# DVE's second layer norm in the MLP phase: eight tensor-scalar operations of 96 columns in place of two broadcast operations

## What is computed

```python
def _ln(x, g, b):
    m = jnp.mean(x, axis=-1, keepdims=True)
    v = jnp.mean(jnp.square(x - m), axis=-1, keepdims=True)
    return (x - m) * jax.lax.rsqrt(v + EPS) * g + b
xs = jnp.roll(x, shift=(-SHIFT, -SHIFT), axis=(1, 2))
# win: xs in windows, (windows, 64 tokens, 96)
h = _ln(win, ln1_g, ln1_b)
q, k, v = (jnp.einsum('ntc,chd->nthd', h, w) + b for w, b in ((wq, bq), (wk, bk), (wv, bv)))
attn = jax.nn.softmax(jnp.einsum('nqhd,nkhd->nhqk', q, k) / np.sqrt(KD), axis=-1)
win = win + jnp.einsum('nqhd,hdc->nqc', jnp.einsum('nhqk,nkhd->nqhd', attn, v), wo) + bo
h2 = _ln(win, ln2_g, ln2_b)
win = win + jax.nn.gelu(h2 @ w1 + b1, approximate=False) @ w2 + b2
# and back: windows to image, roll by (+SHIFT, +SHIFT)
```

## Time and profile before

| what | value |
|---|---|
| time of 3 runs | 5121.0, 5121.04, 5125.81 us; median 5121.04 us |
| span of the profiled execution | 5118.4 us, 275139 instructions |
| PE busy | 4931.8 us (96%), 103124 instructions |
| PEld busy | 4154.1 us (81%) |
| DVE busy | 4072.6 us (80%), 9254 instructions |
| ACT busy | 3873.0 us (76%) |
| POOL busy | 3623.5 us (71%) |
| DMA | 410.68 MB, mean 80 GB/s |

### The profile page before, as it was taken

The page is one execution under the profiler, slowest core; times in us unless marked ns, Lnnn a source line. Parts: engine busy times, 40 slices in busy tenths (PEclk is TensorE's granted clock), DMA queues, the critical chain, the costliest instruction groups (busy, mean ns, idle before and its releaser), DMA issues.

```text
span 5118.4 us, 275139 instructions
## 1 busy us (share of the span) xinstructions
PE 4931.8 (96%) x103124; PEld 4154.1 (81%) x103124; DVE 4072.6 (80%) x9254; ACT 3873.0 (76%) x8206; POOL 3623.5 (71%) x3589
## 2 busy tenths in 40 slices
PE   7999999999999999999999999999999999999999
PEld 6888888888888888888888888887888888888887
DVE  8969778697786977869788796887968879698786
ACT  7859688595886958769587695976949769496794
POOL 6868667686676866767767677676776767777676
PEclk9999999999999999999999999999999999999999
DMA  3141331313213132131322314223042230422304
GB/s 109 34 119 54 94 94 42 116 48 102 86 48 116 42 111 77 56 113 37 117 74 62 112 33 123 68 68 109 26 123 68 74 108 24 124 65 77 108 26 122
DMA packets 222028, 410.68 MB, mean 80 GB/s; under 512 B 29225, under 2 KB 131850, under 8 KB 221898
## 3 DMA queue, kind: packets, MB, share of 16 engines
q1 hardware_dynamic: 220336, 409.06, 27.0%
q10 hardware_dynamic: 1562, 0.50, 0.0%
HBM read 208.11 MB, written 201.33 MB: 80 GB/s over the span
## 4 chain that ended last, share of the span: by engine, by line
PE 55%; DVE 16%; DMA 9%; issue 8%; SPq 7%; ACT 2%; DVEq 2%; POOL 1%; ACTq 0%; POOLq 0%
PE psum L576 12%; PE psum L702 6%; PE psum L591 6%; PE psum L622 6%; PE psum L651 5%; PE psum L608 5%; PE psum L688 5%; PE psum L637 5%; DMA oT<-turned_rows 5%; DMA turned_rows<-normed 4%; SPq L269 4%; PE psum L544 4%; DVE normed L1002 3%; SPq L275 2%; DVE normed L1009 2%
## 5 line engine op out<-in xcount | busy, mean ns | idle before, releaser
L340 POOL TENSOR_TENSOR probs<-probs,prob_inv 128x512 f32<-128x512 f32 x771 | 783.1, 1043 | 839.6 <-DVE prob_inv L982 836.2
L988 DVE TENSOR_TENSOR stream<-stream,psum 128x384 f32 (+1 forms) x1024 | 547.1, 549 | 298.5 <-PE psum L702 225.0
L750 ACT ACTIVATE normed<-stream,shift,rstd 128x96 f32 (+1 forms) x2072 | 770.5, 461 | 17.8 <-issue 16.1
L902 DVE BATCH_NORM_STATS2 stats<-stream 128x6 f32 (+2 forms) x4224 | 721.3, 243 | 58.0 <-DVE stream L988 29.4
L379 POOL TENSOR_TENSOR rstd<-variance,minus_half 128x8 f32<-128x8 f32 (+2 forms) x201 | 745.0, 3707 | 15.7
L347 POOL TENSOR_TENSOR hT<-hT_upper,hT_lower 96x1024 f32<-96x1024 f32 x258 | 614.2, 2380 | 11.8 <-DVE hT_lower L951 6.8
L702 PEld LDWEIGHTS psum<-w_w,gelu_odd 128*64 128x64 f32 x12288 | 512.4, 137 | 59.4 <-issue 59.4
L974 DVE TENSOR_REDUCE prob_sum<-probs 128x8 f32<-128x512 f32 x771 | 492.5, 678 | 84.2 <-ACT probs L784 84.1
L966 DVE TENSOR_TENSOR probs<-psum,row_max 128x512 f32<-128x512 f32 x771 | 533.2, 692 | 26.6
L830 ACT ACTIVATE gelu_odd<-psum 128x512 f32<-128x512 f32 x768 | 418.7, 593 | 174.8 <-PE psum L688 156.5
L702 PE MATMUL psum<-w_w,gelu_odd 128*64 128x96 f32 x12288 | 536.4, 247 | 12.2 <-ACT gelu_odd L830 12.2
(11 more groups left out here) (94 smaller groups left out, 11327.9 us busy)
## 6 DMA issues: line engine op xcount, KB each, us to landing
turned_rows<-normed SPq DMA_DIRECT2D x624, 128.0 KB
stream<-in_x SPq DMA_DIRECT2D x272, 192.0 KB
out<-stream SPq DMA_DIRECT2D x256, 192.0 KB
stream<-in_x SPq DMA_DIRECT2D x272, 180.0 KB
out<-stream SPq DMA_DIRECT2D x256, 180.0 KB
probsT<-turned_rows SPq DMA_DIRECT2D x112, 384.0 KB, 3.2
oT<-turned_rows SPq DMA_DIRECT2D x112, 384.0 KB, 3.2
turned_rows<-gelu_odd SPq DMA_DIRECT2D x144, 128.0 KB
```

What stands on the lines that cost most here:

```text
L340: nc.gpsimd.tensor_tensor(block_h, block_h, inv, ALU.mult).then_inc(probs_ready, 1)
L750: last = nc.scalar.activation(normed1[:, t, :], stream[:, slot, t * C:(t + 1) * C], ACT.Identity, bias=shift1[:, index, t:t + 1], scale=rs ...
L902: last = nc.vector.bn_stats(stats[:, index, c, :], stream[:, slot, c * C:(c + 1) * C])
L988: nc.vector.tensor_tensor(part, part, psum[:, banks[g], 0:GROUP], ALU.add).then_inc(added, 1)
```

## The change

In `normalise2` of DVE the two operations over 768 columns become eight `tensor_scalar` operations, one for each tile of 96 columns. Each reads its tile of the stream and does both steps, subtraction of the mean and multiplication by rstd, with two operands of one value for each partition. `scale2`, its wait and the semaphore `centre2_step` are gone; `ln2_ready` is incremented by the last of the eight. POOL's own `normalise2`, for units 0 to 2, is as before. The number of DVE's instructions for a unit's norm goes from two to eight; nothing else changes on any engine.

```diff
-        centre2_step = sem("centre2_step")
...
                 wait_apart(dve, h2_turned, u)
                 dve.wait_ge(rstd2_ready, u + 1)
-                nc.vector.tensor_tensor(normed2[:, :, :],
-                                        stream[:, slot_of(u), :].rearrange("p (t c) -> p t c", c=C),
-                                        mean2[:, index, :].unsqueeze(2).to_broadcast((P, TILES, C)),
-                                        ALU.subtract).then_inc(centre2_step, 1)
-
-            def scale2(b, u, index):
-                dve.wait_ge(centre2_step, (BATCH - AHEAD) * b + index - AHEAD + 1)
-                nc.vector.tensor_tensor(normed2[:, :, :], normed2[:, :, :],
-                                        rstd2[:, index, :].unsqueeze(2).to_broadcast((P, TILES, C)),
-                                        ALU.mult).then_inc(ln2_ready, 1)
+                for t in range(TILES):
+                    last = nc.vector.tensor_scalar(
+                        normed2[:, t, :], stream[:, slot_of(u), t * C:(t + 1) * C],
+                        mean2[:, index, t:t + 1], rstd2[:, index, t:t + 1], ALU.subtract, ALU.mult)
+                last.then_inc(ln2_ready, 1)
...
                     normalise2(batch + j + 3, j + 3)
-                    scale2(b, batch + j + 3, j + 3)
                     turn_h2(batch + j + 3, turned_late, False)
```

## The result

The changed kernel takes 5209.83 us (median of 4 runs, 5206.17 to 5217.93) against 5121.51 of the kernel before (median of 4): ratio 1.0173, 95% interval 1.0159 to 1.0188. Its profiled execution took 5206.17 us, with a span of 5201.9, 83.5 us more than the span before.

The account below looks back on a forecast made before the run. TensorE was taken to bound the MLP phases, losing time to DVE's late lower half and ACT's gelu. Unit 11's 0.7 us over 16 phases gave 11 us off 5121: 5110 us, range 5073 to 5140.

Parts of the forecast that it names:

- the rival "slower": GpSimd's additions delay norms uncovered, pushing odd units up to unit 11: 5134 us, 5125 to 5150; chance 26%.
- (b): GpSimd's addition gets in among the eight; DVE waits 1.83 us; hand-off in units 6 and 8 about 3.4, 1.1 more.
- hand-off: Time from the norm's start to the transpose's start; 2.30 us in quiet unit 6 before the change.
- decision points: Hand-offs of 3.2 us in unit 6 and 3.9 in unit 8, from which odd units are pushed, up to unit 11.
- The cover: Slack to hide (b) in unit 6: lower half ready at 2167.13, TensorE asks for it at 2170.17.
- (a): A norm behind a running GpSimd operation has its instructions prepared meanwhile: 0.4 us less in units 3, 9 and 15.
- The number 0.237: Estimated us between starts of the eight on DVE, set by its sequencer's register operations; bounds 0.158 and 0.29.
- the 2.27 us: Forecast hand-off in a quiet unit, against 2.30 before; bounds 1.7 and 2.65; no gain there.
- (c): GpSimd's small statistics steps stop waiting: queue 1.3 us earlier behind units 5, 7, 10; some 0.6 left at unit 11.
- Unit 11: One tensor-scalar, two GpSimd operations, seven tensor-scalars; transpose at 2200.7 instead of 2201.40, 0.7 us per phase.
- The "much faster" rival: DVE's own pace holds, or unit 11 is interrupted once: 31 us off, 5090 us (5070 to 5098); chance 30%.
- the signs named: Expected trace marks, such as 0.24 us pace; wrong if GpSimd waits for all eight or TensorE waits at units 7 to 9.

Follow-up runs that it names:

- e6: Changed kernel with mean and rstd at an index that does not depend on the loop (right statistics left out for units 4 to 15): 5200.7 us, ratio 1.0143.
- e8: Changed kernel with two constants in place of the per-partition mean and rstd: 5121.86 us, ratio 1.0001 to the kernel before.
- e2: Changed kernel with the old two broadcast operations back in even units 4 to 14, the eight in odd units: 5165.39 us, ratio 1.0073.
- e1: Changed kernel, but the eight write normed2 with a one-element gap after every 32 columns: 5054.84 us, ratio 0.9859 to the kernel before.
- e7: Changed kernel with a gap after every 48 columns of normed2 (two parts; output not right): 5206.06 us, ratio 1.0168.
- e10: Changed kernel with GpSimd's lower half done on all 128 partitions instead of 96 (output not right): 5193.44 us, ratio 1.0133.

## The prediction against the runs

**Direction and range were wrong.** 5110 us (5073 to 5140) was forecast, 5209.83 measured; the rival "slower" had 5125 to 5150.

**The step that failed is (b).** That a GpSimd operation would get in among the eight was right, at 1.85 us for 2.52, and that it arrives as the norm begins. It was priced as one addition, 1.83 us of waiting, a hand-off of 3.4. But the earlier trace rows was read one row too short. Behind the addition of unit 6 GpSimd has two more operations ready, in the kernel before as well:

```profile
2153.30 2.52 POOL L436 TENSOR_TENSOR stream<-stream,b_all 128x768 f32 x1 [0.44 <-POOL rstd L379]
2155.79 1.28 POOL L429 TENSOR_TENSOR h2T_even_lower<-probsT,h2T_even_upper 96x512 fp32r<-96x512 f32 x1
2157.03 1.83 POOL L436 TENSOR_TENSOR stream<-stream,b_all 128x768 f32 x1
```

and unit 11 in the earlier trace rows had already shown such a pair go ahead of a waiting DVE operation, for 3.62 us. Together they make 1.83 + 1.25 + 1.83 = 4.9 us, and a hand-off of 6.65 us. So the decision points of the "slower" rival, 3.2 us in unit 6 and 3.9 in unit 8, were passed by 3.5 and 0.2 us; that (b) is not covered was the rival's mechanism, but its price in unit 6 was 4.3 us above quiet, where the forecast had 1.1 and the rival 1.8, and the rival saw the loss pass through the odd units to unit 11, where TensorE first stands still at unit 6 itself.

**The cover was too thin, and measured in the wrong queue.** 3.0 us lay between lower half and matmul; a loss of 4.3 goes through it by 1.3, and TensorE waited 1.88 us. It waited for gelu_odd, since ACT comes to its copy first, in order: the cover should have been counted there too.

**Unit 14 was in no step.** It rose from 2.91 to 6.55 us by the same three operations. DVE makes the lower half of unit 13 behind this norm, and so come the stalls at 114 us: 27.5 us of waiting for the odd lower half, where 2.4 stood.

**(a) was nearly nothing.** Unit 3 went from 3.82 to 3.74 us, not by 0.4: after a release the operations start 0.24 us apart as ever, since the pace is not that of the sequencer's register operations. Unit 9 went from 3.63 to 3.57. Unit 15 did fall, from 4.19 to 2.35, but not by (a): none of its eight is held up in any phase, since GpSimd's operations no longer meet them. The number 0.237 was right for a wrong reason (e6, e8): that was luck, and so was the 2.27 us that rests on it.

**(c) was right, and was harm.** GpSimd's two small steps of the earlier trace rows hardly wait any more. Their groups over the run, in the columns of the earlier trace rows:

```profile
L363 POOL TENSOR_TENSOR gap_square<-mean_gap 128x32 f32<-128x32 f32 x80 | 20.2, 252 | 0.0
...
L366 POOL TENSOR_SCALAR spread<-spread 128x32 f32<-128x32 f32 x80 | 17.5, 219 | 6.7
```

The means were 568 and 472 ns before. The prediction knew that this brings GpSimd to the norm's start, and took it as a gain at unit 11. e2 shows that it hurts the old form as well.

**Unit 11** was to be transposed 0.7 us earlier, and its hand-off rose from 5.78 to 6.03. The order was nearly as described: one tensor-scalar, then one that waits 3.10 us for both GpSimd operations, six more; but the start gains nothing by (a).

**Left out: the clock.** The granted clock falls to half, the 1.2 GHz level, right behind some of the new stalls. TensorE waits 2.08 us for the odd lower half until 2267.66, and then three stretches have (columns as in the earlier trace rows, the clock third from the end)

```profile
2265.50:2269.10 3.60, 1.52 (x7) 1.24 (x7) 3.60 (x7) 1.02 (x3) 1.37 (x1) 1.00 0.47 124
2269.20:2272.50 3.30, 3.30 (x30) 2.56 (x30) 3.06 (x13) 0.00 (x0) 0.00 (x0) 0.50 0.66 200
2272.70:2276.00 3.30, 3.30 (x74) 3.14 (x71) 1.38 (x4) 2.53 (x5) 1.21 (x1) 1.00 0.25 73
```

Matmuls of one shape show what that costs, two of the first stretch and two of the second:

```profile
2268.43 0.39 PE L687 MATMUL psum<-h2T_odd_upper,w_split_upper 128*128 128x512 f32 x1
2268.66 0.40 PE L687 MATMUL psum<-h2T_odd_upper,w_split_lower 128*128 128x512 f32 x1
...
2269.50 0.63 PE L687 MATMUL psum<-h2T_odd_upper,w_split_lower 128*128 128x512 f32 x1
2269.92 0.63 PE L687 MATMUL psum<-h2T_odd_lower,w_split_upper 128*128 128x512 f32 x1
```

They start 0.42 us apart instead of 0.23. In the MLP phases the record of the clock has 11 such stretches, 37.5 us together, all of them behind one of the three stalls; before, it had 3 there, 10.2 us. At half speed the 27.3 us more are some 13.7 us of lost work, half of the 27 by which TensorE is busy longer in these phases. No run takes the other half apart. So the 83.5 us of the span are 64 of idle TensorE and 27 of longer busy time in the MLP phases, less some 7 in the rest of the run.

**The "much faster" rival** had the right idea of what is to be won but made it too small. It took 31 us from the best phase before; e1, where no norm waits at all, shows 136.4 us for the mean phase, 3.7 below the mean before, and 73 us in all.

Of the signs named, these were right: 0.24 us in quiet units, one fused and one single register operation each, additions of 1.83 us, near 10 us of waiting for gelu_even (11.7). Not right: about 2 us of gap in units 6 and 8 (unit 6 takes 4.3 more than a quiet one), GpSimd's small steps all below 0.3 us (two of them still take 0.31 and 0.33 in the mean), and 20 us of waiting for the lower halves (55.1). TensorE waits at the start of unit 6 and, in 10 of 16 phases, again at one of the units 7 to 9: the sign that was named for a wrong prediction.

## What to carry to other kernels

Before a long vector operation is cut into short ones that share SBUF with another engine, count everything that engine has ready at that moment, not the one operation that collides: each opening lets one in, and a queue that got faster arrives earlier. If the short ones are wanted, see whether they can run without the shared access at all; a few hundredths of a microsecond more for each (0.365 for 0.32 us) bought 155 us here.

## What the runs showed of the hardware

- A tensor-scalar of 96 fp32 columns starts every 0.24 us and takes 0.32 with two operands per partition, 0.13 and 0.20 to 0.22 with two constants (e8).
- With outermost dimensions of 3 and 96 it takes 0.365 us, 0.28 apart, and neither waits for GpSimd nor holds it up (e1); with 2 and 96 it takes 0.32 us and waits for GpSimd as in the changed kernel (e7).
- The side that waits gets SBUF at the end of the other's operation, even where that other has its next one ready; but an addition on 128 partitions behind a lower half on 96 went ahead of a waiting DVE operation (3.10 us), and no longer did with 128 for both (1.32 and 1.86 us, e10). The cause is open.
